# A decoder layer on one core: B by state from B by token, the norms' last step on ScalarE, split loads, products of ones in the fill, and new orders

## The reference

```python
# 1. state space mixing: 16 heads of 16 channels, 64 states
logA = W_logA x + b_logA                  # per head and token
X, B, C = split(silu(W_XBC x + b_XBC))    # 16, 64 and 64 columns per head
Y[i] = sum over j <= i of exp(cum[i] - cum[j]) * (C[i] . B[j]) * X[j]
x = norm(x + ((W_gate x + b_gate) * Y) @ W_out.T + b_out)
# 2. cross attention to 77 masked context rows, 16 heads
x = norm(x + softmax(q k' / 4) v @ proj_w + proj_b)
# 3. FFN with 1024 hidden units
x = norm(x + relu(x @ W1 + b1) @ W2 + b2)
```

## Time and profile before

| | |
|---|---|
| three runs | 693.05, 692.83, 691.18 us; median 692.83 |
| profiled execution | 689.68 us, span 687.9 us, mean granted clock 0.97 |
| busy share of the span | PE 91%, PEld 77%, DVE 78%, ACT 66%, POOL 70% |
| DMA | 79.2 MB, 115 GB/s on the mean, q1 41.5% of 16 engines |
| chain that ended last | PE 60%, DVE 19%, ACT 6%, POOL 4%, issue 4%, DMA 3%, SPq 3% |

### The profile page before, as it was taken

One profiled execution on the slowest core, in us unless ns is written; L12 is line 12 of the kernel. 1 busy time (PEld: TensorE's weight loads), 2 busy tenths in 40 slices (PEclk: granted clock), 3 DMA queues, 4 the chain that ended last, 5 costly groups with the idle time before them and its releaser, 6 DMA issues.

```text
span 687.9 us, 21922 instructions
## 1 busy us (share of the span) xinstructions
PE 623.0 (91%) x8266; PEld 530.8 (77%) x8266; DVE 539.6 (78%) x1325; ACT 452.7 (66%) x1105; POOL 483.3 (70%) x774
## 2 busy tenths in 40 slices
PE   2797787879999999999999999999999999988976
PEld 2566565658888888888888888888888788878875
DVE  2365789897989888888889798888888798987341
ACT  4576776777777776877777877878687774323321
POOL 1234756756879687787877796878777778776775
PEclk9599899999999999999999999999999999998999
DMA  6112436444444344444544444444454434445410
GB/s 235 57 39 45 112 100 178 105 131 124 119 119 131 100 119 116 135 125 126 137 106 118 124 132 109 121 111 130 121 138 125 124 91 114 131 110 153 132 34 29
DMA packets 91126, 79.20 MB, mean 115 GB/s; under 512 B 47373, under 2 KB 85645, under 8 KB 91021
## 3 DMA queue, kind: packets, MB, share of 16 engines
q1 hardware_dynamic: 90173, 76.31, 41.5%
q10 hardware_dynamic: 848, 1.49, 0.6%
HBM read 43.37 MB, written 33.55 MB: 112 GB/s over the span
## 4 chain that ended last, share of the span: by engine, by line
PE 60%; DVE 19%; ACT 6%; POOL 4%; issue 4%; DMA 3%; SPq 3%; DVEq 0%; POOLq 0%; ACTq 0%
PE bank L489 10%; PE bank L477 9%; PE bank L353 8%; PE bank L297 5%; PE bank L466 4%; PE bank L456 3%; DVE E L968 3%; PE bank L425 3%; PE bank L414 3%; DVE rc L1098 3%; PE bank L443 2%; DVE mx L1088 2%; PE bank L367 2%; DVE P L1090 2%; PE bank L309 2%
## 5 line engine op out<-in xcount | busy, mean ns | idle before, releaser
L1300 POOL TENSOR_TENSOR P<-P,rc 128x308 f32<-128x308 f32 x128 | 86.9, 708 | 27.2 <-DVE rc L1102 27.2
L736 ACT ACTIVATE E<-bank 128x512 f32<-128x512 f32 x128 | 68.2, 600 | 26.1 <-PE bank L340 25.9
L1324 POOL TENSOR_TENSOR hl<-hr,hh 128x512 fp32r<-128x512 f32 x64 | 81.7, 1279 | 2.7
L968 DVE TENSOR_TENSOR E<-bank,E 128x512 f32<-128x512 f32 x128 | 80.3, 677 | 4.1 <-POOL E L1260 3.2
L788 ACT ACTIVATE hr<-bank,cst 128x256 f32<-128x256 f32 x128 | 57.6, 490 | 36.7 <-PE bank L477 29.6
L489 PE MATMUL bank<-w2h,hh 128*128 128x256 f32 x256 | 75.1, 293 | 5.7 <-POOL hl L1324 5.7
L1260 POOL TENSOR_SCALAR_AFFINE_SELECT E<-E 128x508 f32<-128x508 f32 x128 | 79.5, 645 | 0.0
L1269 POOL TENSOR_SCALAR st<-st 128x1 f32<-128x1 f32 x96 | 21.6, 225 | 78.6 <-DVE st L1022 78.4
L353 PE MATMUL bank<-Cc,Bc 64*128 64x128 f32 x1024 | 72.9, 288 | 1.0 <-DVE cst L951 0.3
L353 PEld LDWEIGHTS bank<-Cc,Bc 64*128 64x128 f32 x1024 | 63.4, 193 | 12.8 <-issue 8.8
L489 PE MATMUL bank<-w2l,hh 128*128 128x256 f32 x256 | 71.7, 280 | 0.0
(11 more groups left out here) (112 smaller groups left out, 1745.6 us busy)
## 6 DMA issues: line engine op xcount, KB each, us to landing
turn_p<-TP SPq DMA_DIRECT2D x128, 160.0 KB, 2.8
PT<-turn_p SPq DMA_DIRECT2D x32, 640.0 KB, 4.0
xr<-in_x SPq DMA_DIRECT2D x32, 128.0 KB, 2.4
turn_x<-xr SPq DMA_DIRECT2D x128, 32.0 KB, 1.7
tT<-turn_x SPq DMA_DIRECT2D x32, 128.0 KB, 2.1
turn_x<-x SPq DMA_DIRECT2D x128, 32.0 KB, 1.6
xu<-turn_x SPq DMA_DIRECT2D x32, 128.0 KB, 2.2
out<-res SPq DMA_DIRECT2D x32, 128.0 KB, 2.1
```

The costliest lines, as they stand in the source:

```text
L736: eng.activation(E[:, h % 4, r, :, :], b_diff[n, u, r][:, :].rearrange("p (h t) -> p h t", h=4), ACT.Exp).then_inc(decay_exp, 1)
L968: eng.tensor_tensor(E[:, h % 4, r, :, :], b_g[n, u, r][:, :].rearrange("p (h t) -> p h t", h=4), E[:, h % 4, r, :, :], ALU.mult).then_inc( ...
L1300: eng.tensor_tensor(v, v, rc[:, n % 2, 4 * j:4 * j + 4].unsqueeze(2).to_broadcast([128, 4, S]), ALU.mult).then_inc(p_norm, 1)
L1324: eng.tensor_tensor(hl[:, 2 * j:2 * j + 2, :], hr[:, j % 2, :, :], hh[:, 2 * j:2 * j + 2, :].bitcast(F), ALU.subtract).then_inc(h_rest, 1)
```

## The change

- `bc` makes C alone. B by state comes from B by token: VectorE's `b_blocks` transposes the 32 x 32 blocks of `Bt` into `TB`, `put_b` writes them to DRAM by four DMAs, `get_b` reads them back into `Bc`, which has three buffers, one per tile, and holds the eight pairs of heads next to each other. `gmat`'s stationary operand is therefore read with a step of eight words. ScalarE's `tok` waits for the transpose before it writes the buffer of `Bt` again.
- `norm_out` goes from VectorE to ScalarE, as one activation with scale and bias; GpSimd's `rstd` has a third instruction, which makes that bias.
- `cst` keeps 27 columns; its three matrices are a load of their own (`cmat`) on SP. The context operands go from ScalarE's queue to SP's, behind the first tiles' work, and so do `w3` and `b3`.
- `warm` issues eight products of ones by ones, 512 columns each, at six places in TensorE's fill.
- The orders of all five engines are new: fill, turn and end.

```diff
+        d4 = nc.dram_tensor("turn_b", (2, 4, 32, 4, 256), F, kind="Internal").ap()
-        cst = sb("cst", [128, 35 + 3 * 128])
+        cst = sb("cst", [128, 27])
+        cmat = sb("cmat", [128, 3 * 128])
-        Bc = sb("Bc", [128, 2, 8, GW])
+        Bc = sb("Bc", [128, 3, 4, 32, 8])
+        TB = sb("TB", [128, 4, 32, 8])
...
# TensorE, gmat
-                pe.wait_ge(bc_silu, 16 * (g + 1))
+                pe.wait_ge(bc_silu, 8 * (g + 1))
+                pe.wait_ge(b_T[n % 2], DMA * (n // 2 + 1))
...
-                        i = eng.matmul(b_g[n, u, r][:, 128 * q:128 * q + 128], Bc[k, g % 2, 2 * q + u, cols(n)],
+                        i = eng.matmul(b_g[n, u, r][:, 128 * q:128 * q + 128], Bc[k, n % 3, :, :, 2 * q + u],
                                        Cc[k, g % 2, 2 * q + u, cols(n)], start=True, stop=True)
...
+            def warm(k):
+                bk = banks.take(pe, warm_mm, k + 1)
+                pe.wait_ge(ones, 1)
+                for _ in range(8):
+                    i = eng.matmul(bk[:, 0:512], onesr[:, :], onesr[:, :].unsqueeze(1).to_broadcast([128, 4, 128]),
+                                   start=True, stop=True)
+                i.then_inc(warm_mm, 1)
...
# ScalarE, tok and the norms
+                act.wait_ge(b_flip, n - 2)
...
+            def norm_out(k, n, r):
+                s_ = st[:, k, n % 2, :]
+                act.wait_ge(ln_nmr[k], n + 1)
+                eng.activation(r, r, ACT.Identity, bias=s_[:, 8:9], scale=s_[:, 9:10]).then_inc(ln_out[k], 1)
...
# VectorE
+            def b_blocks(n):
+                if not is_tile(n):
+                    return
+                if n:
+                    dve.wait_ge(b_put[(n - 1) % 2], 4 * DMA * ((n - 1) // 2 + 1))
+                dve.wait_ge(tokb_silu, 4 * n + 4)
+                eng.transpose(TB[:, :, :, :].rearrange("x j b p -> x p j b"),
+                              Bt[:, n % 3, :].rearrange("x (p j b) -> x p j b", p=8, j=4)).then_inc(b_flip, 1)
...
-                eng.tensor_scalar(r, r, s_[:, 6:7], s_[:, 9:10], ALU.subtract, ALU.mult).then_inc(ln_out[k], 1)
...
# GpSimd, rstd
                 eng.tensor_tensor(s_[:, 9:10], s_[:, 8:9], mhalf, ALU.pow).then_inc(ln_rstd[k], 1)
+                pool.wait_ge(ln_rstd[k], n + 1)
+                eng.tensor_scalar(s_[:, 8:9], s_[:, 6:7], s_[:, 9:10], -1.0, ALU.mult, ALU.mult).then_inc(ln_nmr[k], 1)
...
# SP
+            def put_b(n):
+                if not is_tile(n):
+                    return
+                sp.wait_ge(b_T[n % 2], DMA * (n // 2))
+                sp.wait_ge(b_flip, n + 1)
+                for i in range(4):
+                    eng.dma_start(d4[n % 2, :, :, i, :].rearrange("j a c -> a j c"),
+                                  TB[32 * i:32 * i + 32, :, :, :].rearrange("x j b p -> x j (b p)")).then_inc(b_put[n % 2], DMA)
+
+            def get_b(n):
+                if not is_tile(n):
+                    return
+                sp.wait_ge(g_mm, 4 * (n - 2))
+                sp.wait_ge(b_put[n % 2], 4 * DMA * (n // 2 + 1))
+                eng.dma_start(Bc[:, n % 3, :, :, :].rearrange("x i b p -> x (i b p)"),
+                              d4[n % 2].rearrange("j a i c -> (j a) (i c)")).then_inc(b_T[n % 2], DMA)
```

More of the change, by code:

```diff
@@ L555, in _ @@
+            gmat(2, 1)
+            inter(2)
+            diff(3, 1)
             cum(4)
             ecum(3)
-            inter(2)
+            query(0)
+            score(0)
             state_in(2)
-            query(0)
-            ecum(4)
[L561 to L566, removed]
+            gate(2)
+            diff(4, 0)
+            y(2)
+            warm(5)
+            diff(4, 1)
+            tok(5)
@@ L583, in _ @@
[L583 to L598, removed]
-            for s in range(4, 18):
+            tok(6)
+            y(3)
+            for s in range(4, 18):
+                inter(2 * s - 5)
+                gmat(2 * s - 4, 0)
+                gate(2 * s - 5)
+                cum(2 * s - 2)
+                bc(s - 1)
+                ffn1(s - 6, range(3, 6))
+                out_proj(2 * s - 5)
+                gmat(2 * s - 4, 1)
+                pv(2 * s - 8)
+                inter(2 * s - 4)
+                state_in(2 * s - 4)
+                query(2 * s - 6)
+                attn_proj(2 * s - 8)
+                diff(2 * s - 3, 0)
+                score(2 * s - 6)
@@ L612, in _ @@
[L612 to L615, removed]
+                ffn2(2 * s - 12)
+                state_turn(2 * s - 4)
+                ecum(2 * s - 3)
+                out_proj(2 * s - 4)
+                cum(2 * s - 1)
+                state_in(2 * s - 3)
+                pv(2 * s - 7)
+                query(2 * s - 5)
+                attn_proj(2 * s - 7)
+                diff(2 * s - 2, 0)
+                diff(2 * s - 2, 1)
@@ L625, in _ @@
[L625 to L639, removed]
@@ L640, in _ @@
-                y(2 * s - 2)
+            gate(31)
+            inter(31)
+            ffn1(12, range(3, 6))
+            out_proj(31)
+            pv(28)
+            query(30)
+            attn_proj(28)
+            score(30)
+            ffn1(12, range(6, 8))
+            ffn2(24)
+            ffn2(25)
             query(31)
-            ffn1(12, range(6, 8))
             score(31)
             pv(29)
-            ffn2(24)
+            ffn1(13, range(0, 3))
             attn_proj(29)
-            ffn2(25)
@@ L863, in _ @@
+                ln2_out(2 * s - 6)
                 exp_diff(2 * s - 1, 1)
-                hidden(s - 5, range(3, 6))
                 p_soft(2 * s - 4)
+                u_top(2 * s - 8)
+                tok(2 * s + 1)
+                ecum(2 * s - 1)
+                state_turn(2 * s - 2)
+            u_top(27)
             query(31)
-            hidden(12, range(6, 8))
-            u_top(26)
+            ln3_out(24)
+            ln3_out(25)
             o_turn(29)
+            hidden(13, range(0, 3))
@@ L945, in log_a @@
                     return
+                dve.wait_ge(ld_cmat, DMA)
                 dve.wait_ge(cum_mm, n)
@@ new lines, in _ @@
+            rows(6)
+            load_x(4)
+            load_resid(5)
+            put_x2(0)
+            get_x1(3)
+            get_b(6)
+            load_w(3)
+            put_p(2)
+            put_x1(4)
+            put_b(7)
+            rows(7)
+            get_p(2)
+            get_x1(4)
+            put_x2(1)
+            load_resid(6)
+            get_b(7)
+            get_x2(0)
+            put_p(3)
+            put_x1(5)
+            for s in range(4, 17):
+                put_b(2 * s)
+                get_p(2 * s - 5)
+                put_x2(2 * s - 6)
```

662 lines of the change are left out of this document (345 added, 317 removed).

## The result

The changed kernel takes 740.62 us (median of four runs, 737.48 to 740.91) against 692.00 (four runs, 690.26 to 693.05): 1.0695 times as long, 95% interval 1.0657 to 1.0733. Forecast were 669 and a range up to 712. Its profiled execution took 740.77 us, with a span of 738.9.

What follows compares the result with a forecast made beforehand. The prediction took TensorE, 98.8% busy in the middle 360 us, as the bound. Its terms, -13.7 (B's products), 0, -5 (fill) and -5 (orders), took 689.68 to 666.0, with 3.15 added 669 us; range 652 to 712.

Steps and rivals of the forecast that it cites:

- the stationary operand of C times B: Weight loads of `gmat` on TensorE, columns now 32 bytes apart: taken as 0, with +54 us as the far end.
- first rival: Stepped weight loads on TensorE cost more and cannot hide: 707 to 723 us, say 715; chance 0.20.
- VectorE's write: VectorE's transpose writing with a step of 8 words: 1.22 us per tile, at most 2.4; cost to the path 0.
- second rival: VectorE becomes the bound, 34.0 us per turn, a turn of 37.8 if 90% busy: 684 us; chance 0.14.
- B's products: One call a turn, 1.08 us, leaves TensorE: 10.3 us in the middle, 3.4 elsewhere, sum -13.7.
- Fill: Start of the kernel: first product of C and B at 21.5 to 23.5 us, before 26.46; -5, ends 0 and -9.
- 16 us of slack: B's way from Bt to Bc takes 10 to 12 us, VectorE's transpose stands 27 us ahead of its reader: cost 0.
- New orders: TensorE's idle time at the end and from 40 to 180 us, 44.5 us: -5, ends +8 and -15.
- the ring: From 40 to 180 us, four TensorE banks fewer per turn ease it; counted within the -5 for orders.
- The forecast's own range: Whole kernel, from the ends of fill and orders: 652 to 682 us around 669; the forecast's chance was 0.52.
- the DMAs for B: Per tile four writes and one read through DRAM, landing 2.8 and 4.0 us after issue: cost 0.
- ScalarE's step: Norms' last step on ScalarE, 406 to 494 ns each; with B's activations gone, a gain of 1 to 10 us, hidden.

## Why the prediction was wrong

| spans, us | to y(8) | y(8) to y(31) | behind | in all |
|---|---|---|---|---|
| before | 175.0 | 430.6 | 82.3 | 687.9 |
| after | 187.9 | 468.8 | 82.2 | 738.9 |
| TensorE reads adjacent columns | 183.9 | 433.9 | 81.3 | 699.1 |
| VectorE writes them so too | 181.7 | 423.3 | 79.6 | 684.6 |
| no DMAs for B | 176.4 | 422.4 | 80.7 | 679.5 |
| no transposes for B | 171.5 | 422.5 | 79.7 | 673.6 |

- **The step that failed** is the stationary operand of C times B: "I take 0, the rate of its own row". The row had adjacent columns, and its rate said nothing about a step. A load takes 329 ns instead of 193, and adjacent columns for the loads alone gave 39.6 us back. The far end of the term, 54, was close (55.4 in the old kernel with the step alone), by two errors against each other: a load's extra is 136 ns and not 105, so that a call's 1.01 us over 64 calls is 64.6; but TensorE has idle time that takes up some of it, 7.8 us in the old kernel with the step. The first rival was the mechanism, and it had 0.20. It was also the one case of which the trace said that its cost could not hide, since the load is the longest thing in each pair.
- **VectorE's write** was bounded rightly (2.1 us of at most 2.4), and "0 either way as long as TensorE covers it" fits the middle of the changed kernel, where TensorE is full, though it was not tried by itself there. Once the loads are cheap it is not 0 but 14.8 us. The second rival was sized well, but as an alternative to the first; both were true, one behind the other. The figure of the Trainium skill, "Vector Engine (DVE) Microarchitecture Reference", section 5.2, 2.50 ns a column at a step of 24 words, is of the right size: 2107 ns over 1024 columns are 2.06 at eight words here.
- **B's products**, -13.7: even in the kernel with B's way taken out, the stretch behind tile 8 gives 430.6 - 422.5 = 8.1 us over 11.5 turns, 0.7 a turn and not 1.08. In that stretch the products of C and B, with adjacent columns, took 53.5 us, before 50.2: 3.3 more, 0.3 a turn. Why, and the other 0.1, stay open.
- **Fill**, -5: tile 0's `y` came 4.9 us earlier, which meets the forecast by luck. The first product of C and B, where my sum ended, started at 25.9, not at 21.5 to 23.5: 0.5 us earlier than before. The rest was gained behind it, where I had summed nothing. By tile 8 it was lost: without either step `y(8)` is 6.6 us late, of which B's way is 10.2. The "16 us of slack" for B was taken from the turn and does not exist in the first tiles, where TensorE idles and the chain runs through VectorE and DMAs. These rows of the changed kernel's chain show a transpose for B standing on it.

```profile
50.27 1.15 PE bank L419 x4
52.53 2.04 DVE TB L1006
55.38 0.74 DVE x L973 x2
```

- **New orders**, -5 for the end and the ring: the end gave 2.7 us without either step and nothing in the changed kernel; the ring was not measured by itself.
- **The forecast's own range** was summed wrongly: the ends of fill (0, -9) and orders (+8, -15) around 669 are 655 and 687, not 652 and 682.
- **Right**: the DMAs for B land in 2.4 and 3.7 us (2.8 and 4.0 taken) and no wait of `gmat` for them shows, though the get of P now lands after 4.8 instead of 4.0; ScalarE and GpSimd stay below VectorE (61% and 68% of the span busy), though ScalarE's step at 602 to 614 ns makes it 9.7 us more work where I had summed 1 to 10 less; the signs by which I wanted to know the first rival (loads over 250 ns, calls near 2 us) are the ones that came.

## What to carry to other kernels

Where an edit changes how an operand lies in memory, the duration of the same instruction on another layout is no estimate for it: bound it by more than twice the time of its columns (here 105 ns of columns grew by 136), and if that engine is the full one, give that case the larger chance. For fp32 a step of 8 bytes was as good as none here and one of 16 already paid in full, on the reading and the writing side. A layout that cures the step also changes the run length of DMAs and the shape of their source: look at both. Work that is free in the steady part of a kernel should be priced once more in the fill, with the fill's own chain.

## What the runs showed of the hardware that was not expected

- A load of 128 fp32 columns into TensorE takes 191 to 203 ns at steps of 4 and 8 bytes, 324 to 330 at 16 and 32. VectorE's transpose of 128x1024 has the same edge: 1234 to 1248 and 2076 to 2107 ns. ScalarE's activation of 128x256 went from 494 to 737 ns at 32 bytes.
- The same 128 packets of 4 KB took 2.3 us where the get's source was one dimension of 128 pieces and 6.7 to 6.8 us where it was 4 by 32, 3.8 to 3.9 under way on the mean instead of 11.3. A load behind it landed after 8.6 to 8.7 us instead of 4.0.
- With runs of 128 bytes instead of 1 KB, and that slower get, puts of P of unchanged size landed after 4.1 us instead of 2.8.
- An activation of 128x256 from SBUF to SBUF with scale and bias as columns takes 602 to 614 ns, more than the silu with a bias out of PSUM (494).
- With products of ones the granted clock of the first 40 us was 0.83 instead of 0.74 in the old fill, and 2.5 us were gained; in the new fill, taking them out changed nothing that can be measured in the time, and the granted clock there was 1.00 without them and 0.83 with them.
